# A retention and gated feed-forward block in fp32: the state update as four fp32 products, behind the scores

## The chip, the cores and the metric
The kernel runs on one core of one Trainium2 chip. Its metric is the device time of one execution in microseconds (us). TensorE (PE) multiplies, VectorE (DVE), ScalarE (ACT) and GpSimd (POOL) do the elementwise work, SyncE (SP) issues the DMAs.

## The reference, cut to what matters
Eight sequences of 512 tokens, 256 wide, go through a retention layer and a feed-forward layer, each with a residual and a layer norm. Retention has four heads, keys of 64 and values of 128. The reference works in chunks of 64 tokens; the state is what the change is about:

```python
attn = jnp.einsum('bhid,bhjd->bhij', qb, kb) * D[None]
o_intra = jnp.einsum('bhij,bhjd->bhid', attn, vb)
o_inter = jnp.einsum('bhid,bhde->bhie', qb * cross_q, S)
S_new = gC * S + jnp.einsum('bhjd,bhje->bhde', kb * cross_k, vb)
```

q and k are rotated (rotary embedding) first. The retained output is normed per head, gated with silu(x Wg), multiplied by Wo, added to x and layer-normed to x1. Then silu(x1 Wgate) * (x1 Wup) is multiplied by Wdown, added to x1 and layer-normed.

## The kernel before
**Tiling.** A tile is 128 tokens, four to a sequence, 32 in all. The decay factors are folded into the rotary tables, so that the state of a sequence is a plain sum of k^T v over its tiles. Every engine walks the same slots s = 0, 1, 2, ... (`walk_and_drain`), and in slot s it does the projections of tile s, the scores and retained products of tile s-1, the output projection of tile s-2, and the feed-forward of older tiles. Slots 0 to 11 and the last four are written out, the others are a loop over sequences; slots 0 to 7 (`natural`) also make q by rows, and 8 and later make it by columns. After slot 31 comes a `drain` for what is left. The order within a slot is written out by hand for each engine, and semaphores join the engines; within an engine all is in order.

**Split products.** Most products have each operand in two parts of type fp32r, high and low, and are the sum of three products high-high, high-low, low-high (`split_product`, whose matmul is L440). ScalarE casts the high part and GpSimd or VectorE subtracts to get the low part. Other products take fp32 operands as they are: the recall of the state (L555) and the scores (L558), both with 64 rows of contraction, and the retained products (L587), with 128. The profile shows each fp32 product as two pairs of weight load and matmul.

**The state.** `b_state` is a PSUM bank in which the update of a sequence accumulates over its first three tiles (the fourth has nobody to pass it to), 24 updates in all. Two heads share a product of 128 stationary columns of k and 256 columns of v, and only the diagonal halves of the result are used. So there are two pairs of heads by three split products, at the head of `to_projections` for tile s-2. `split_kv` casts k and v to `k_hi` and `v_hi` on ScalarE (L873, L874), and GpSimd makes `k_lo` and `v_lo` (L1516, L1517). `keep_state` on ScalarE copies the two diagonal halves into `state` (L925). The recall of the next tile waits for that (`state_kept`), and also for `y_ready` of the tile before its own, since it writes the PSUM banks that VectorE's `gated_output` reads (L1316). The v and k buffers have two slots each; who overwrites them waits for `kv_split`.

**PE's order in a slot** is: first projection, state update, feed-forward block 1, down projection, second projection, feed-forward block 2, recall and scores, transposes of x1 (L576) and of y (L615), gate projection (L454, L458), feed-forward block 0, output projection, retained products (L587), transposes of q and k (L468). Block 0 waits for the low part of x1 transposed (L1295) and the output projection for that of y (L1304), both made by VectorE from what ScalarE has cast (L885, L903).

Of the kernel before, what the change touches and what calls it, by code (L numbers as in the profile page):

```python
# [77 lines left out]
def build_block(nc, xT, x, w_proj, w_o, gn, w_ffn, rope, rope_by_row, out):  # L78
# [6 lines left out]
    with ExitStack() as ctx:  # L85
        def sb(name, shape, dt=F32):
            return ctx.enter_context(nc.sbuf_tensor(name, shape, dt))
# [4 lines left out]
        def sem(name):  # L92
            return ctx.enter_context(nc.semaphore(name))
# [13 lines left out]
        v_sb = sb("v_sb", [P, 2, V])  # L107
        v_hi, v_lo = sb("v_hi", [P, V], F32R), sb("v_lo", [P, V], F32R)

# [28 lines left out]
        qkT = sb("qkT", [P, 4, P])  # L138
        k_hi, k_lo = sb("k_hi", [P, 256], F32R), sb("k_lo", [P, 256], F32R)
        attn = sb("attn", [P, H, P])  # L140
# [84 lines left out]
        v_copied, g_gated = sem("v_copied"), sem("g_gated")  # L225
        kv_high, kv_split = sem("kv_high"), sem("kv_split")
        scores_done, masked = sem("scores_done"), sem("masked")
# [185 lines left out]
        def _(pe):  # L413
# [178 lines left out]
            def update_state(s, q, t):  # L592

                n, (qn, tn) = s - 2, back(q, t, 2)
                if exists(n) and tn < TS - 1:
                    if tn == 0 and exists(n - 2):
                        pe.wait_ge(state_kept, states_to(qn, tn) - 1)
                    pe.wait_ge(kv_split, states_to(qn, tn))
                    for pr in range(2):
                        cols, vals = slice(pr * P, (pr + 1) * P), slice(pr * 256, (pr + 1) * 256)  # L600
                        mm = split_product(b_state[:, vals], [(k_hi[:, cols], k_lo[:, cols])],
                                           [(v_hi[:, vals], v_lo[:, vals])], begun=(tn > 0 or pr > 0),
                                           more=(tn < TS - 2))
                    mm.then_inc(state_done, 1)
# [88 lines left out]
            def to_projections(s, q, t, wide):  # L693
                q1, t1 = q, t - 1
                update_state(s, q, t)
                gate_up_block(s - 1, q1, t1, 1, wide)
                down(s - 1, q1, t1, wide)
                if natural(s):
                    project(s, q, t, 1, v_done)
                else:  # L700
                    keys_and_queries(s, q, t)
                if is_slot(s, 0):
                    warm(FILL)
                gate_up_block(s - 1, q1, t1, 2, wide)
                recall_and_score(s, q, t)
                turn_x1(s, q, t)
                turn_y(s, q, t)
                project(s, q, t, 2, g_done)
# [18 lines left out]
            def drain(wide):  # L727

                q = NSEQ
                at = lambda t: (NT + t, q, t)  # L730
                update_state(*at(0))
                gate_up_block(*at(-1), 1, wide)
# [64 lines left out]
        def _(act):  # L797
# [58 lines left out]
            def copy_v(s, q, t):  # L856

                if exists(s):
                    act.wait_ge(v_done, s + 1)
                    if exists(s - 2):  # L860
                        act.wait_ge(o_done, s - 1)

                        act.wait_ge(kv_split, states_to(*back(q, t, 2)))
                    act.copy(v_sb[:, t % 2], v_bank(s, t)[:]).then_inc(v_copied, 1)

            def split_kv(s, q, t):

                if exists(s) and t < TS - 1:
                    act.wait_ge(rotated, s + 1)
                    act.wait_ge(v_copied, s + 1)  # L870
                    if exists(s - 1):
                        act.wait_ge(state_done, states_to(*back(q, t, 1)))
                    act.copy(k_hi[:], qk[:, t % 2, 256:512])  # L873
                    act.copy(v_hi[:], v_sb[:, t % 2]).then_inc(kv_high, 1)  # L874

# [42 lines left out]
            def keep_state(s, q, t):  # L918

                qn, tn = back(q, t, 1)  # L920
                if exists(s - 1) and tn < TS - 1:
                    act.wait_ge(state_done, states_to(qn, tn))
                    for a in range(2):
                        rows = slice(a * DK, (a + 1) * DK)
                        last = act.copy(state[rows], b_state[rows].rearrange(  # L925
                            "p (c n) -> p c n", c=2)[:, :, a * DV:(a + 1) * DV])
                    last.then_inc(state_kept, 1)

# [45 lines left out]
            def steady_slot(s, q, t):  # L974
# [6 lines left out]
                split_h(s - 1, t - 1, 0)  # L981
                split_kv(*prev)
                split_h(s - 1, t - 1, 1)
# [18 lines left out]
            def slot(s, q, t, ahead):  # L1002
# [17 lines left out]
                if is_slot(s, 1):  # L1020
                    split_xT(s + 2, *back(q, t, -2))
                    copy_v(s, q, t)
                    split_kv(s - 1, *back(q, t, 1))
                    split_ffn(0)
                elif is_slot(s, FFN_LAG) or is_slot(s, FFN_LAG + 1):
                    split_xT(s + 2, *back(q, t, -2))
                    copy_v(s, q, t)
                    if is_slot(s, FFN_LAG):
                        sum_low_ffn(3)
                    else:  # L1030
                        split_h(s - 1, t - 1, 1)
                        keep_x1(s, q, t)
                        split_kv(s - 1, *back(q, t, 1))
                else:
                    keep_x1(s, q, t)
                    split_h(s - 1, t - 1, 1)
                    split_kv(s - 1, *back(q, t, 1))
                    if ahead:
                        split_xT(s + 2, *back(q, t, -2))
                    copy_v(s, q, t)  # L1040
# [61 lines left out]
        def _(dve):  # L1102
# [59 lines left out]
            def rotate(s, q, t):  # L1162

                if exists(s):
# [3 lines left out]
                    if exists(s - 2):  # L1168
                        dve.wait_ge(qkT_done, s - 1)
                        dve.wait_ge(kv_split, states_to(*back(q, t, 2)))  # L1170
                    for e, sign in ((0, ALU.subtract), (1, ALU.add)):
# [28 lines left out]
            def sum_k(s, q, t):  # L1200

                if exists(s):
# [4 lines left out]
                    dve.wait_ge(qkT_done, s - 1)  # L1207
                    dve.wait_ge(kv_split, states_to(*back(q, t, 2)))
                    for e, sign in ((0, ALU.subtract), (1, ALU.add)):
# [270 lines left out]
        def _(pool):  # L1480
# [30 lines left out]

            def split_kv(s, q, t):

                if exists(s) and t < TS - 1:
                    pool.wait_ge(kv_high, states_to(q, t))
                    pool.tensor_tensor(k_lo[:], qk[:, t % 2, 256:512], k_hi[:].bitcast(F32), ALU.subtract)  # L1516
                    pool.tensor_tensor(v_lo[:], v_sb[:, t % 2], v_hi[:].bitcast(F32), ALU.subtract).then_inc(kv_split, 1)  # L1517

            def rms_norm(s, q, t):
# [37 lines left out]
            def steady_slot(s, q, t):  # L1557
# [3 lines left out]
                split_h(s - 1, t - 1, 0)  # L1561
                split_kv(*prev)
                split_h(s - 1, t - 1, 1)
# [7 lines left out]
            def slot(s, q, t, ahead):  # L1571
# [7 lines left out]
                split_h(s - 1, t - 1, 1)  # L1579
                split_kv(*before)  # L1580
                if ahead:
# [67 lines left out]
```

## Time and profile before

| | us |
|---|---|
| median of 3 runs | 443.9 (443.34 to 444.12) |
| profiled execution, its own time | 444.02 |
| its span, first to last instruction | 442.2 |
| PE busy (matmuls) | 428.2, 97% |
| PE weight loads | 400.4, 91% |
| VectorE busy | 302.1, 68% |
| ScalarE busy | 295.7, 67% |
| GpSimd busy | 238.9, 54% |

In the chain that ended last PE has 85% of the span, VectorE 8%, and 3% are time in which the engine waited for nothing that the profile shows. A row of the trace is one group of instructions in order of time: its start, its length, the engine, the line of the kernel, what is written and read, the tile of the array (rows*columns), the shape, the count, and in brackets the idle time before it and what ended it. Matmuls overlap, so that the length of one (0.27 to 0.28 us) is longer than the step from one to the next (0.11 us); the cost of a group is the step from its start to the start of the next.

### The profile page before, as it was taken

The page shows a single profiled execution, that of the slowest core. Times are in us where ns is not written, and L with a number is a line of the kernel's source. Part 1 is how long each engine was busy: PE and PEld are TensorE (multiplying, and loading weights), DVE is VectorE, ACT ScalarE, POOL GpSimd, SP SyncE. Part 2 cuts the span into 40 slices and gives each one's busy share as a digit, 9 for nine tenths or more (in the row PEclk, how much of TensorE's full clock was granted, in tenths as well). Part 3 has the DMA queues.
Part 4 walks back from the last instruction along what each step waited for, and adds up shares of the span by engine and source line. Part 5 has one row for each costly group of instructions (what it writes and reads, how often), then busy time and mean ns, then how long its engine had stood idle before and what let it go on. Part 6 is the DMA issues. An engine that isn't in the chain of part 4 may idle for free.

```text
span 442.2 us, 10997 instructions
## 1 busy us (share of the span) xinstructions
PE 428.2 (97%) x3552; PEld 400.4 (91%) x3552; DVE 302.1 (68%) x857; ACT 295.7 (67%) x891; POOL 238.9 (54%) x381
## 2 busy tenths in 40 slices
PE   7989999999999999999999999999999999999994
PEld 3878889999999999999999999999999999999983
DVE  4989566657766776666776667677666667766774
ACT  5678766657766767765776676686676667665541
POOL 2654255755555465453766446564655546554564
PEclk9999999999999999999999999999999999999998
DMA  7931000011100111110111101011110000100011
GB/s 241 363 134 50 0 29 22 24 38 37 38 11 27 37 38 38 37 37 0 36 36 36 36 27 44 0 36 36 36 36 13 15 22 14 38 12 13 14 38 39
DMA packets 16228, 19.60 MB, mean 44 GB/s; under 512 B 1472, under 2 KB 13760, under 8 KB 16192
## 3 DMA queue, kind: packets, MB, share of 16 engines
q1 hardware_dynamic: 16192, 19.14, 13.2%
q8 instruction: 20, 0.33, 0.3%
q14 instruction: 16, 0.13, 0.1%
HBM read 14.94 MB, written 4.19 MB: 43 GB/s over the span
## 4 chain that ended last, share of the span: by engine, by line
PE 85%; DVE 8%; issue 3%; POOL 1%; ACT 1%; DMA 1%; SPq 0%; POOLq 0%; DVEq 0%; ACTq 0%
PE b_rows L440 28%; PE b_ffn L440 18%; PE b_rows L458 8%; PE b_rows L454 6%; PE b_head L587 6%; PE b_head L555 3%; PE b_state L440 3%; PE b_head L558 3%; PE b_turn L615 3%; PE b_ffn L576 2%; PE b_turn L468 2%; DVE y L1316 1%; DMA wf_int<-in_w_proj 1%; DVE qk L1172 1%; DVE rot_s L1159 1%
## 5 line engine op out<-in xcount | busy, mean ns | idle before, releaser
L1509 POOL TENSOR_TENSOR h_lo<-wf_int,h_hi 128x256 fp32r<-128x256 f32 x96 | 71.0, 740 | 76.5 <-ACT h_hi L951 76.2
L440 PE MATMUL b_ffn<-x1T_hi,wf_hi 128*128 128x256 f32 x384 | 93.2, 279 | 1.0 <-DVE x1T_lo L1295 1.0
L440 PE MATMUL b_ffn<-x1T_lo,wf_hi 128*128 128x256 f32 x384 | 92.5, 278 | 0.0
L440 PEld LDWEIGHTS b_ffn<-x1T_hi,wf_hi 128*128 128x128 f32 x384 | 72.2, 188 | 2.1 <-DVE x1T_lo L1295 1.6
L440 PEld LDWEIGHTS b_ffn<-x1T_lo,wf_hi 128*128 128x128 f32 x384 | 72.3, 188 | 0.3
L915 ACT ACTIVATE sq<-b_head 128x128 f32<-128x128 f32 x124 | 34.4, 277 | 54.7 <-PE b_head L587 51.7
L1534 POOL TENSOR_TENSOR ve<-mv,eps 128x1 f32<-128x1 f32 x64 | 14.2, 222 | 93.7 <-DVE mv L1337 87.3
L940 ACT ACTIVATE wf_int<-b_ffn 128x256 f32<-128x256 f32 x96 | 36.8, 383 | 32.8 <-PE b_ffn L440 32.6
L951 ACT CAST h_hi<-wf_int 128x256 fp32r<-128x256 f32 x96 | 38.8, 405 | 19.1 <-DVE wf_int L1249 18.2
L1328 DVE TENSOR_TENSOR z<-b_rows,x_sb 128x256 f32<-128x256 f32 x32 | 13.5, 423 | 55.4 <-PE b_rows L440 55.4
L1249 DVE TENSOR_TENSOR wf_int<-b_ffn,wf_int 128x256 f32<-128x256 f32 x96 | 40.1, 418 | 15.5 <-ACT wf_int L940 11.2
L440 PE MATMUL b_rows<-wf_hi,h_hi 128*128 128x256 f32 x192 | 45.6, 278 | 0.3 <-POOL h_lo L1509 0.3
L440 PE MATMUL b_rows<-wf_hi,h_lo 128*128 128x256 f32 x192 | 45.3, 277 | 0.0
L1316 DVE SCALAR_TENSOR_TENSOR y<-b_head,rms,g_sb 128x128 f32<-128x128 f32 x124 | 34.9, 343 | 10.4 <-POOL rms L1528 9.9
L1536 POOL TENSOR_TENSOR rs<-ve,half_neg 128x1 f32<-128x1 f32 x64 | 34.9, 545 | 5.0
L1528 POOL TENSOR_TENSOR rms<-ms_eps,half_neg 128x4 f32<-128x4 f32 x32 | 36.0, 1124 | 2.5
L440 PE MATMUL b_rows<-wo_hi,yT_hi 128*128 128x256 f32 x128 | 35.7, 279 | 1.1 <-DVE yT_lo L1304 1.1
L440 PEld LDWEIGHTS b_rows<-wf_hi,h_hi 128*128 128x128 f32 x192 | 36.1, 188 | 0.5 <-POOL h_lo L1509 0.5
L440 PEld LDWEIGHTS b_rows<-wf_hi,h_lo 128*128 128x128 f32 x192 | 36.1, 188 | 0.0
L458 PE MATMUL b_rows<-wp_hi,xT_lo 128*128 128x256 f32 x144 | 36.0, 277 | 0.0
L440 PE MATMUL b_rows<-wo_lo,yT_hi 128*128 128x256 f32 x128 | 35.4, 276 | 0.0
L440 PE MATMUL b_rows<-wo_hi,yT_lo 128*128 128x256 f32 x128 | 35.4, 276 | 0.0
(154 smaller groups left out, 1320.2 us busy)
## 6 DMA issues: line engine op xcount, KB each, us to landing
xT_raw<-in_xT SPq DMA_DIRECT2D x16, 256.0 KB, 3.1
x_sb<-in_x SPq DMA_DIRECT2D x16, 256.0 KB, 2.7
out<-wf_int SPq DMA_DIRECT2D x32, 128.0 KB, 1.7
wf_int<-in_w_ffn SPq DMA_DIRECT2D x6, 384.0 KB, 7.6
wf_int<-in_w_proj SPq DMA_DIRECT2D x6, 256.0 KB, 5.2
rope_sb<-in_rope SPq DMA_DIRECT2D x4, 256.0 KB, 6.6
rope_q<-in_rope_by_row SPq DMA_DIRECT2D x2, 512.0 KB, 9.4
wo_raw<-in_w_o SPq DMA_DIRECT2D x1, 512.0 KB, 6.8
```

Of the source, the lines that this page charges most:

```text
L440: mm = pe.matmul(dst, a, b, start=(i == 0 and j == 0 and not begun), stop=(i == n - 1 and j == len(passes) - 1 and not more), skip_group_c ...
L454: pe.matmul(dst[:], a, b, start=i == 0, stop=False, skip_group_check=True)
L458: mm = pe.matmul(dst[:, cols], a, b[:, cols], start=False, stop=i == n - 1, skip_group_check=True)
L587: mm = pe.matmul(o_of(n, h), attn[:, h, :], v_sb[:, tn % 2, h * DV:(h + 1) * DV], start=False, stop=True, skip_group_check=True)
L915: act.activation(sq[:], o_of(n, h), ACT.Square, scale=float(DV) ** -0.5, accum_out=ms[:, tn % 2, h:h + 1]).then_inc(squared, 1)
L940: act.activation(act_g[:, u], b_ffn[u][:, 0:256], ACT.Silu, scale=SCALE).then_inc(silu_done[j], 1)
L951: act.copy(h_hi[:, ((t - FFN_LAG) // 2) % 2, hb], h_full[:, u]).then_inc(h_high[j], 1)
L1249: dve.tensor_tensor(h_full[:, u], b_ffn[u][:, 256:512], act_g[:, u], ALU.mult).then_inc(h_ready[j], 1)
L1316: last = dve.scalar_tensor_tensor(y[:, cols], o_of(n, h), rms[:, tn % 2, h:h + 1], g_sb[:, tn % 2, cols], ALU.mult, ALU.mult)
L1509: pool.tensor_tensor(h_lo[:, ring, hb], h_full[:, u], h_hi[:, ring, hb].bitcast(F32), ALU.subtract).then_inc(h_split[j], 1)
L1528: pool.tensor_tensor(rms[:, tn % 2], ms_eps[:, tn % 2], half_neg[:], ALU.pow).then_inc(rms_ready, 1)
L1536: pool.tensor_tensor(rs, ve, half_neg[:, 0:1], ALU.pow).then_inc(rstd, 1)
```

## The change
The state update becomes four fp32 products, one for each head: 128 rows, the head's 64 columns of k as the stationary operand, its 128 columns of v moving. The output of head h goes to partitions 0 to 63 or 64 to 127 (`half(h)`) and to the left or right 128 columns of what it uses of the bank. It is issued behind `recall_and_score` of the same slot for tile s-1, where it was issued at the head of the slot for tile s-2. `split_kv` is gone on both engines with its four tiles and two semaphores. `keep_state` is one copy of 128 partitions instead of two of 64. Where `kv_split` guarded the buffers of k and v, `state_done` does.

```diff
             def update_state(s, q, t):
 
-                n, (qn, tn) = s - 2, back(q, t, 2)
+                n, (qn, tn) = s - 1, back(q, t, 1)
                 if exists(n) and tn < TS - 1:
                     if tn == 0 and exists(n - 2):
                         pe.wait_ge(state_kept, states_to(qn, tn) - 1)
-                    pe.wait_ge(kv_split, states_to(qn, tn))
-                    for pr in range(2):
-                        cols, vals = slice(pr * P, (pr + 1) * P), slice(pr * 256, (pr + 1) * 256)
-                        mm = split_product(b_state[:, vals], [(k_hi[:, cols], k_lo[:, cols])],
-                                           [(v_hi[:, vals], v_lo[:, vals])], begun=(tn > 0 or pr > 0),
-                                           more=(tn < TS - 2))
+                    pe.wait_ge(rotated, n + 1)
+                    pe.wait_ge(v_copied, n + 1)
+                    for h in range(H):
+                        mm = pe.matmul(b_state[half(h), (h // 2) * DV:(h // 2 + 1) * DV],
+                                       qk[:, tn % 2, 256 + h * DK:256 + (h + 1) * DK],
+                                       v_sb[:, tn % 2, h * DV:(h + 1) * DV],
+                                       start=(tn == 0 and h < 2), stop=tn == TS - 2, skip_group_check=True)
                     mm.then_inc(state_done, 1)
...
             def to_projections(s, q, t, wide):
                 q1, t1 = q, t - 1
-                update_state(s, q, t)
                 gate_up_block(s - 1, q1, t1, 1, wide)
...
                 recall_and_score(s, q, t)
+                update_state(s, q, t)
                 turn_x1(s, q, t)
...
-                        act.wait_ge(kv_split, states_to(*back(q, t, 2)))
+                        act.wait_ge(state_done, states_to(*back(q, t, 2)))
                     act.copy(v_sb[:, t % 2], v_bank(s, t)[:]).then_inc(v_copied, 1)
-
-            def split_kv(s, q, t):
-
-                if exists(s) and t < TS - 1:
-                    act.wait_ge(rotated, s + 1)
-                    act.wait_ge(v_copied, s + 1)
-                    if exists(s - 1):
-                        act.wait_ge(state_done, states_to(*back(q, t, 1)))
-                    act.copy(k_hi[:], qk[:, t % 2, 256:512])
-                    act.copy(v_hi[:], v_sb[:, t % 2]).then_inc(kv_high, 1)
...
                 if exists(s - 1) and tn < TS - 1:
                     act.wait_ge(state_done, states_to(qn, tn))
-                    for a in range(2):
-                        rows = slice(a * DK, (a + 1) * DK)
-                        last = act.copy(state[rows], b_state[rows].rearrange(
-                            "p (c n) -> p c n", c=2)[:, :, a * DV:(a + 1) * DV])
-                    last.then_inc(state_kept, 1)
+                    act.copy(state[:], b_state[:, 0:2 * DV].rearrange("p (c n) -> p c n", c=2)).then_inc(state_kept, 1)
...
-            def split_kv(s, q, t):
-
-                if exists(s) and t < TS - 1:
-                    pool.wait_ge(kv_high, states_to(q, t))
-                    pool.tensor_tensor(k_lo[:], qk[:, t % 2, 256:512], k_hi[:].bitcast(F32), ALU.subtract)
-                    pool.tensor_tensor(v_lo[:], v_sb[:, t % 2], v_hi[:].bitcast(F32), ALU.subtract).then_inc(kv_split, 1)
```

In the drain the update of tile 30, which stood at its head, is likewise gone: slot 31 does it. VectorE's `rotate` and `sum_k`, which write k, wait for `state_done` of the tile two before instead of `kv_split`.

## Rows read from the trace of the kernel before

**Rows 1.** The page: busy time by engine, and granted clock in 40 slices.
```profile
PE 428.2 (97%) x3552; PEld 400.4 (91%) x3552; DVE 302.1 (68%) x857; ACT 295.7 (67%) x891; POOL 238.9 (54%) x381
...
PEclk9999999999999999999999999999999999999998
```

**Rows 2.** The timeline, PE, of slot 19: first of six update products, and next block.
```profile
236.13 0.28 PE L440 MATMUL b_state<-v_hi,k_hi 128*128 128x256 f32 x1
...
236.81 0.28 PE L440 MATMUL b_ffn<-x1T_hi,wf_hi 128*128 128x256 f32 x1
```

**Rows 3.** The timeline, PE: retained products of a tile, and what follows.
```profile
233.64 1.05 PE L587 MATMUL b_head<-v_sb,attn 128*128 128x128 f32 x8
...
234.53 0.38 PE L468 MATMUL b_turn<-ident,qk 128*128 128x128 f32 x2
```

**Rows 4.** The timeline, PE: last feed-forward product, recall, scores, x1 transposes.
```profile
241.26 0.28 PE L440 MATMUL b_ffn<-x1T_lo,wf_hi 128*128 128x256 f32 x1
...
241.47 0.71 PE L555 MATMUL b_head<-state,qT 64*128 64x128 f32 x8
...
242.02 0.61 PE L558 MATMUL b_head<-qT,qkT 64*128 64x128 f32 x8
...
242.56 0.44 PE L576 MATMUL b_ffn<-ident,x 128*128 128x128 f32 x2
```

**Rows 5.** The timeline, a steady slot: y, and the scores that wait for it.
```profile
264.75 1.12 DVE L1316 SCALAR_TENSOR_TENSOR y<-b_head,rms,g_sb 128x128 f32<-128x128 f32 x4 [0.45 <-POOL rms L1528]
...
267.41 0.72 PE L558 MATMUL b_head<-qT,qkT 64*128 64x128 f32 x8
```

**Rows 6.** The timeline of slot 4: y, the rotation's additions, the recall.
```profile
43.73 1.11 DVE L1316 SCALAR_TENSOR_TENSOR y<-b_head,rms,g_sb 128x128 f32<-128x128 f32 x4
...
44.77 0.75 DVE L1172 TENSOR_TENSOR qk<-rot_c,rot_s 128x256 f32<-128x256 f32 x2
...
45.20 0.71 PE L555 MATMUL b_head<-state,qkT 64*128 64x128 f32 x8 [1.04 <-DVE y L1316]
```

**Rows 7.** The timeline at the head of the drain: y, and the last recall.
```profile
406.58 1.13 DVE L1316 SCALAR_TENSOR_TENSOR y<-b_head,rms,g_sb 128x128 f32<-128x128 f32 x4 [0.96 <-POOL rms L1528]
...
407.92 0.71 PE L555 MATMUL b_head<-state,qT 64*128 64x128 f32 x8
```

**Rows 8.** By tile, ns min/median/max, first and last start: removed casts, split and copy.
```profile
L873 ACT CAST k_hi<-qk x24: 401/408/437, 16.4 to 394.8; 128x256 fp32r<-128x256 f32 x24
...
L874 ACT CAST v_hi<-v_sb x24: 613/622/648, 16.8 to 395.1; 128x512 fp32r<-128x512 f32 x24
L1517 POOL TENSOR_TENSOR v_lo<-v_sb,v_hi x24: 1267/1296/1731, 18.2 to 396.5; 128x512 fp32r<-128x512 f32 x24
...
L925 ACT COPY state<-b_state x48: 365/368/372, 21.7 to 405.7; 64x256 f32<-64x256 f32 x48
```

**Rows 9.** The timeline of slot 2: PE's two stalls, and what VectorE and GpSimd do.
```profile
24.21 1.27 POOL L1517 TENSOR_TENSOR v_lo<-v_sb,v_hi 128x512 fp32r<-128x512 f32 x1
24.63 2.00 DVE L1172 TENSOR_TENSOR qk<-rot_c,rot_s 128x256 f32<-128x256 f32 x2
...
24.77 0.66 PE L615 MATMUL b_turn<-ident,y 128*128 128x128 f32 x4 [0.57 <-DVE y L1316]
...
26.43 0.40 PE L440 MATMUL b_rows<-wp_hi,xT_lo 128*128 128x512 f32 x1
...
27.95 0.39 PE L440 MATMUL b_rows<-wo_hi,yT_hi 128*128 128x256 f32 x1 [1.12 <-DVE yT_lo L1304]
```

**Rows 10.** The timeline of slot 5: the cast of v, and PE's stall.
```profile
58.53 0.62 ACT L874 CAST v_hi<-v_sb 128x512 fp32r<-128x512 f32 x1
...
59.92 0.40 PE L440 MATMUL b_rows<-wp_hi,xT_lo 128*128 128x512 f32 x1
...
60.93 0.39 PE L440 MATMUL b_ffn<-x1T_hi,wf_hi 128*128 128x256 f32 x1 [0.61 <-DVE x1T_lo L1295]
```

**Rows 11.** The timeline of slot 9: PE's stall.
```profile
113.74 0.38 PE L440 MATMUL b_ffn<-x1T_hi,wf_hi 128*128 128x256 f32 x1 [0.37 <-DVE x1T_lo L1295]
```

More of the change, by code:

```diff
@@ L107, in build_block @@
         v_sb = sb("v_sb", [P, 2, V])
-        v_hi, v_lo = sb("v_hi", [P, V], F32R), sb("v_lo", [P, V], F32R)
         state = sb("state", [P, 2, DV])
@@ L138, in build_block @@
         qkT = sb("qkT", [P, 4, P])
-        k_hi, k_lo = sb("k_hi", [P, 256], F32R), sb("k_lo", [P, 256], F32R)
         attn = sb("attn", [P, H, P])
@@ L225, in build_block @@
         v_copied, g_gated = sem("v_copied"), sem("g_gated")
-        kv_high, kv_split = sem("kv_high"), sem("kv_split")
         scores_done, masked = sem("scores_done"), sem("masked")
@@ L730, in drain @@
                 at = lambda t: (NT + t, q, t)
-                update_state(*at(0))
                 gate_up_block(*at(-1), 1, wide)
@@ L981, in steady_slot @@
                 split_h(s - 1, t - 1, 0)
-                split_kv(*prev)
                 split_h(s - 1, t - 1, 1)
@@ L1022, in slot @@
                     copy_v(s, q, t)
-                    split_kv(s - 1, *back(q, t, 1))
                     split_ffn(0)
@@ L1032, in slot @@
                         keep_x1(s, q, t)
-                        split_kv(s - 1, *back(q, t, 1))
                 else:
@@ L1036, in slot @@
                     split_h(s - 1, t - 1, 1)
-                    split_kv(s - 1, *back(q, t, 1))
                     if ahead:
@@ L1169, in rotate @@
                         dve.wait_ge(qkT_done, s - 1)
-                        dve.wait_ge(kv_split, states_to(*back(q, t, 2)))
+                        dve.wait_ge(state_done, states_to(*back(q, t, 2)))
                     for e, sign in ((0, ALU.subtract), (1, ALU.add)):
@@ L1207, in sum_k @@
                     dve.wait_ge(qkT_done, s - 1)
-                    dve.wait_ge(kv_split, states_to(*back(q, t, 2)))
+                    dve.wait_ge(state_done, states_to(*back(q, t, 2)))
                     for e, sign in ((0, ALU.subtract), (1, ALU.add)):
@@ L1561, in steady_slot @@
                 split_h(s - 1, t - 1, 0)
-                split_kv(*prev)
                 split_h(s - 1, t - 1, 1)
@@ L1579, in slot @@
                 split_h(s - 1, t - 1, 1)
-                split_kv(*before)
                 if ahead:
```

## The prediction, made before the changed kernel ran

> **What bounds the kernel now.** I read the page first. TensorE (PE) is busy for 428.2 of the span of 442.2 us, at the full granted clock in nearly every slice; VectorE, ScalarE and GpSimd are busy for 54 to 68% [rows 1]. So work taken off ScalarE or GpSimd is worth nothing by itself: it counts only where PE waits for them. The profiled execution took 444.02 us, 1.8 us more than its span, and the median of the runs shown is 443.9 us. I sum against the profiled one and take 0.1 us off, which is less than anything below.
>
> Next I read PE's order of time in a steady slot. A product of 128 stationary columns and 256 moving ones in the split type follows the one before it after 0.113 us: six of them, the state update of before, stand from 236.13 to the next block at 236.81, 0.68 us [rows 2]. The weight loads lie beside them. The fp32 products of the retained values (four products, recorded as eight pairs of load and product, 128 stationary and 128 moving columns) stand from 233.64 to 234.53, so 0.89 us, 0.111 us a record [rows 3]. The fp32 products of 64 rows, which alternate between the upper and the lower half of the partitions, are quicker: eight records of the scores take from 242.02 to the x1 transposes at 242.56, where one at a time at 0.111 us they would take 0.89 us; the recall's eight take from 241.47 to 242.02 [rows 4]. Two heads run side by side there, and eight records cost about four steps.
>
> The same rows show what it costs to change the shape of tile. The last product of 128 rows begins at 241.26, would be followed after 0.113 us, and the first of 64 rows begins at 241.47: 0.10 us lost [rows 4]. The recall group also takes 0.55 us where four steps of 0.11 would be 0.44, so its first load is not hidden: another 0.1 us. A change of shape costs about 0.2 us.
>
> **The change part by part.** (1) The six split products go: 0.68 us for each of the 24 tiles that update the state (three of four in eight sequences) [rows 2].
>
> (2) Four fp32 products of 128 rows and 64 stationary columns come, behind the scores. No row of before shows this shape. The output of the even heads lies in partitions 0 to 63 and that of the odd in 64 to 127, so neighbours in the order use different column halves of the array, as the scores' neighbours use different row halves. Ends: if halves of columns run side by side as halves of rows do, the eight records take what the recall takes after a change of shape, 0.55 us [rows 4]. If they don't, they take 0.89 us [rows 3]. The change of shape between scores and x1 transposes exists already; now there are two. The second costs 0.10 us at its leaving edge (its entering edge is in the 0.55): 0.65 us with pairs. At the lower end a load of half the columns is hidden sooner and the group takes 0.55 us in all; at the upper end (no pairs, full change) 0.89 + 0.2 = 1.09 us. I take 0.64 us, nearest to the recall, the one group that is fp32, comes after a change of shape and alternates halves. So 24 x (0.64 - 0.68) = -1.0 us.
>
> On this the Trainium skill, TensorEngine Tiling (Array Packing), Key Properties, says that a change of tiling mode, not of tile, drains the engine; the trace agrees, by the 0.10 us ahead of the recall. TensorE: Matmul & The Clock Gate, Measured speedup vs the span model, gives 2.38 times for three column tiles, about what row tiles give, though it doesn't name fp32 there. The sum above does not use that figure.
>
> (3) The update moves from the head of the slot after next to the middle of the next one. Its waits are for the rotated k and the copied v of the previous tile, both of which are older than the scores, so nothing queues behind them. The recall waits for the kept state, and that now comes a whole slot earlier. ScalarE's next copy of v and VectorE's sum of k, which overwrite what the update reads, now wait for the update itself instead of the splits; it stands a slot ahead of them, so nothing is queued behind those waits. But the recall also waits for VectorE's y of the tile before, and the 0.68 us that stood ahead of it is gone. In the steady slots y has slack: it ends at 265.87 where the scores begin at 267.41, and 1.5 us is the smallest slack of them [rows 5]; 0.68 us comes off that and nothing waits. At two places y is already last. In slot 4 y runs from 43.73 for 1.11 us and PE, idle for 1.04 us, begins the recall at 45.20 [rows 6]. At the head of the drain y ends at 407.71 and the recall begins at 407.92 [rows 7]. There the update stood in the shadow of the wait; y is timed by the previous slot's retained products, which the new update pushes back. So each of the two loses the 0.68 us that part 1 counts as saved: +1.4 us.
>
> (4) ScalarE loses two casts (0.408 and 0.622 us) and one of two copies of the state (0.368 us) a tile, 1.4 us; GpSimd loses 1.296 us and the shorter split of k [rows 8]. Over the kernel that is 34 us of ScalarE and more of GpSimd, nearly all of it hidden. It shows where PE waits, early:
> - Slot 2. PE stands from 26.43 to 27.95 where a product of 512 columns takes about 0.23 us, for VectorE's low part of y, and before that 0.57 us for y itself [rows 9]. VectorE is late because its two additions of the rotation took 2.00 us from 24.63, while GpSimd's split of v ran from 24.21 for 1.27 us; the same two took 0.75 us from 44.77 [rows 6, 9]. Without the split of v I give back the 1.25 us and a little at the stall before: -1.4 us of 1.9. What is late then is the gate projection and the remaining y chain.
> - Slot 5. PE waits until 60.93 for the low part of x1, whose high part ScalarE copies only behind the cast of v at 58.53 and a gate [rows 10]. The wait is about 0.8 us (last product at 59.92, so 1.01 less 0.23). ScalarE is 1.0 us earlier: -0.8 us.
> - Slot 9. 0.37 us of idle before 113.74, for the same part of x1, to which I add the 0.1 us that the product ahead of it ran over its step [rows 11]: -0.5 us.
> Together -2.7 us. Bounds: 0 if another chain takes over at each, -3.2 us if all of it goes.
>
> The Trainium skill, SBUF — State Buffer, Who interferes with whom, states that a VectorE instruction with two inputs in SBUF contends with a GpSimd instruction that reads SBUF. The trace agrees: 2.00 against 0.75 us. The sum takes it from those rows.
>
> **Sum**: 444.0 - 1.0 + 1.4 - 2.7 = 441.7 us; taken from the median 441.6, and I say 441.7.
>
> **The rivals.**
> A. Pairs, but the start gives nothing back: the stalls are VectorE's, and its queue in slots 2 to 5 also holds the weight splits. 444.0 - 1.0 + 1.4 = 444.4 us. For it: y in slot 4 has no relief from this change. Against it: 2.00 against 0.75 us.
> B. Column halves do not run side by side, and no change of shape is paid: 0.89 us an update, 24 x 0.21 = +5.0, with the rest +3.7: 447.7 us. For it: the retained products are fp32 of 128 rows and run one at a time [rows 3]; two column halves want two streams of all 128 rows, where two row halves share one. It decides as soon as an update takes more than 0.74 us, where 24 x 0.06 eats the net gain at the waits.
> C. They don't, and the change of shape is paid: 1.09 us, 24 x 0.41 = +9.8, with the rest +8.5: 452.5 us. This is the one that I fear most, slower by 1.9%.
> D. Weight loads of column tiles are not hidden at all: a record then costs the exposed step at the start of the recall, 0.2 us; 8 x 0.2 + 0.2 = 1.8 us an update, 24 x 1.1 = +27, with the rest 470 us. Against it: in every row of the split products and of rows 3 the load of 128 rows lies beside the product before it. The Trainium skill, TensorE: Matmul & The Clock Gate, Measured speedup vs the span model, says that loads overlap products in flight only where the row group differs, and here it does not differ; by that rule D would come. The trace disagrees with the rule for whole tiles, since steps of 0.113 us leave no room for a load.
>
> **Chances.** Forecast 0.57, A 0.13, B 0.13, C 0.15, D 0.02. The forecast's own range is 439.5 (updates of 0.55 us) to 443.5. The whole range runs to B and what lies around it, 450.0, and leaves out C, D and a small tail, 0.2 together. A difference under 0.2% (0.9 us, so 443.0 to 444.8) can't be told from none here. Faster: 0.57 less a tail of 0.03, 0.54. Same: that tail and most of A, 0.11. Slower: the rest of A, B, C, D, 0.35.
>
> **What would show it.** Eight records of the state update in about 0.55 us with starts in close pairs: pairing right; spread evenly by 0.11: B or C. The step from the last score to the first update and from the last update to the x1 transposes, each some 0.2 us: the drain. An unchanged wait near 45 that grows to about 1.7 us, and the same at the head of the drain: part 3 right. VectorE's rotation at 0.75 us in slot 2, and stalls gone at about 27, 60 and 113: part 4 right. Spans of the steady sequences (16 updates and more) that move by more than 0.3 us each are the pairing and nothing else.

## The result, and the profile after

The changed kernel takes 439.59 us (median of four executions, 439.12 to 439.67) where the kernel before takes 443.62 (four, 443.21 to 444.12): a ratio of 0.9906, interval 0.9894 to 0.9918. It is faster by 0.9%, as forecast in direction, and inside the range, but by 4.0 us where the sum gave 2.3. The profiled execution took 439.12 us, the quickest of its four; the one of before took 444.02, 0.4 us over its median. So 4.9 us lie between the two profiles, and some 0.9 of them is spread between executions.

The page after, the part that answers to [rows 1]:

```profile
PE 424.6 (97%) x3600; PEld 393.6 (90%) x3600; DVE 296.6 (68%) x857; ACT 265.8 (61%) x819; POOL 189.0 (43%) x333
...
PEclk9999999999999999999999999999999999999998
...
PE 92%; DVE 2%; POOL 1%; issue 1%; DMA 1%; ACT 1%; SPq 0%; POOLq 0%; DVEq 0%; ACTq 0%
```

ScalarE has lost 30 us and GpSimd 50, PE 3.6. The third line is the chain that ended last: VectorE's share of it fell from 8 to 2%. The granted clock is what it was.

The state update of a steady slot, PE in order of time, between the last feed-forward products and the x1 transposes; it answers to [rows 2, 4]:

```profile
236.87 0.28 PE L437 MATMUL b_ffn<-x1T_lo,wf_hi 128*128 128x256 f32 x1
237.09 0.72 PE L552 MATMUL b_head<-state,qT 64*128 64x128 f32 x8
237.63 0.61 PE L555 MATMUL b_head<-qT,qkT 64*128 64x128 f32 x8
238.18 0.66 PE L598 MATMUL b_state<-v_sb,qk 128*64 128x128 f32 x8
238.76 0.33 PE L573 MATMUL b_ffn<-ident,x 128*128 128x128 f32 x1
```

The scores still take 0.54 us to the next group, and the update 0.59 to the x1 transposes: this, leaving edge included, is its whole cost. The starts of its eight matmuls are 0, 6, 161, 167, 269, 276, 378 and 386 ns: four close pairs, and 0.20 us behind the last. The recall ahead has the same picture, except that its second pair starts at 213 ns. The view by tile, with min, median and max in ns, shows the difference:

```profile
L598 PEld LDWEIGHTS b_state<-v_sb,qk x192: 132/137/138, 16.2 to 393.2; 128*64 128x64 f32 x192
L598 PE MATMUL b_state<-v_sb,qk x192: 272/273/325, 16.2 to 393.3; 128*64 128x128 f32 x192
L910 ACT COPY state<-b_state x24: 384/395/398, 21.6 to 400.7; 128x256 f32<-128x256 f32 x24
```

A load of 64 columns takes 137 ns where those of 128 columns take 188, and the first step of the group, the one place where a load isn't hidden, is 0.05 us shorter than the recall's.

**Where the time went.** The retained products of a tile follow in both kernels on the same stretch of work, so the shift of their start places the gain. The change of those starts is a staircase: from the tile with number 11 on it falls by 0.28 us in each sequence, exactly, from -3.92 to -5.04 at tile 27. That is three updates that cost 0.093 us less each, and nothing else.

| stretch | shift, us | of it updates | of it waits and stalls |
|---|---|---|---|
| weights arrive, to the first scores | -0.34 | | -0.34 |
| to tile 3 | -1.53 | -0.28 | slot 4's recall +0.59, stalls of slots 1 to 3 -1.84 |
| to tile 7 | -1.17 | -0.28 | slot 5's stall -0.89 |
| to tile 11 | -0.88 | -0.28 | slot 9's stall -0.60 |
| to tile 27 | -1.12 | -1.12 | none |
| to tile 31 | +0.42 | -0.28 | the drain's recall +0.70 |
| rest of the drain | -0.27 | | -0.27 |
| sum | -4.89 | -2.24 | -2.65 |

The two waits that grow, PE, in slot 4 and at the head of the drain; they answer to [rows 6, 7]:

```profile
41.32 0.40 PE L437 MATMUL b_rows<-wp_hi,xT_lo 128*128 128x512 f32 x1
...
41.98 1.11 DVE L1295 SCALAR_TENSOR_TENSOR y<-b_head,rms,g_sb 128x128 f32<-128x128 f32 x4
...
43.35 0.71 PE L552 MATMUL b_head<-state,qkT 64*128 64x128 f32 x8 [1.64 <-DVE y L1295]
```

```profile
402.17 0.28 PE L437 MATMUL b_ffn<-x1T_lo,wf_hi 128*128 128x256 f32 x1
...
403.28 0.72 PE L552 MATMUL b_head<-state,qT 64*128 64x128 f32 x8 [0.82 <-issue]
```

The idle time ahead of slot 4's recall went from 1.04 to 1.64 us, behind the same 1.11 us of y. In the drain the step to the recall went from 0.40 to 1.11 us; y ended at 403.06, so the "issue" of the row is the wait for y all the same.

And slot 2, which answers to [rows 9]:

```profile
23.69 0.75 DVE L1151 TENSOR_TENSOR qk<-rot_c,rot_s 128x256 f32<-128x256 f32 x2
...
25.49 0.69 DVE L1283 TENSOR_TENSOR yT_lo<-b_turn,yT_hi 128x512 fp32r<-128x512 f32 x1 [0.38 <-ACT yT_hi L890]
...
25.84 0.40 PE L437 MATMUL b_rows<-wp_hi,xT_lo 128*128 128x512 f32 x1
...
26.24 0.39 PE L437 MATMUL b_rows<-wo_hi,yT_hi 128*128 128x256 f32 x1
```

VectorE's two additions take 0.75 us where they took 2.00, and the step to the output projection is 0.40 us where it was 1.52. The wait for y ahead of its transposes is gone too: the step from the last score to what follows is 0.20 us, where the transposes followed after 0.85, and the update now stands there. The stalls of [rows 10, 11] are gone.

### The profile page after: what moved, and what is told of

It reads as the page before. It is cut to its first block, busy times and chain, and to the rows that moved or that the text cites. A ratio compares the mean times of both kernels' runs of the same rounds, so it can differ in the third digit from the quotient of the medians.

```text
span 437.3 us, 10954 instructions
## 1 busy us (share of the span) xinstructions
PE 424.6 (97%) x3600; PEld 393.6 (90%) x3600; DVE 296.6 (68%) x857; ACT 265.8 (61%) x819; POOL 189.0 (43%) x333
## 4 chain that ended last, share of the span: by engine, by line
PE 92%; DVE 2%; POOL 1%; issue 1%; DMA 1%; ACT 1%; SPq 0%; POOLq 0%; DVEq 0%; ACTq 0%
PE b_rows L437 32%; PE b_ffn L437 19%; PE b_rows L455 9%; PE b_rows L451 6%; PE b_head L584 6%; PE b_head L555 4%; PE b_head L552 3%; PE b_state L598 3%; PE b_turn L613 3%; PE b_ffn L573 2%; PE b_turn L465 2%; DMA wf_int<-in_w_proj 1%; POOL h_lo L1488 1%; DVE wf_lo L1096 0%; POOL rs L1508 0%
```

## Experiments: why an update costs 0.59 us

The prediction's mechanism was: two column halves of the array run side by side, as two row halves do, and a change of tile shape costs 0.2 us. Its reading of how was that the half must alternate from one product to the next. The expectations below number the theories: under Theory 1 alternation of neighbours is what makes the pairs. Its rival is that the pairs do not hang on the order.

**e1: the same products in another order.** Heads 0 and 2 go to the upper partitions, 1 and 3 to the lower, so neighbours now change half once instead of three times.

```diff
-                    for h in range(H):
+                    for h in (0, 2, 1, 3):
```

> The changed kernel with one line altered: the four update products go out in the order of heads 0, 2, 1, 3, so that neighbours share a half of the array's columns, where before they alternated. Theory 1 (the pairs in the trace are two heads side by side in the two halves of columns): heads 0 and 2 run one after the other, so do 1 and 3, and only one meeting of halves is left; the group of eight records grows from 0.59 us by two to three steps of 0.11 us, to 0.8 to 0.9 us, 24 x 0.27 = +6.5 us, 446 us. Rival 2 (the two records that lie 7 ns apart belong to one and the same product): the order of heads does not matter, 0.59 us and 439.6 us.

Measured: 439.69 us, 0.9907 of before (0.9888 to 0.9926). The update's rows:

```profile
238.21 0.67 PE L598 MATMUL b_state<-v_sb,qk 128*64 128x128 f32 x8
238.80 0.44 PE L573 MATMUL b_ffn<-ident,x 128*128 128x128 f32 x2
```

It takes 0.59 us as before, and the starts still come in pairs: 0, 14, 160, 175, 270, 284, 379 and 393 ns. Theory 1 missed by 6 us. The only thing that changed is the distance inside a pair, 14 ns instead of 7. This fits two streams, one for each half, each in its own order: in the new order the first matmul of the second half is the fourth behind the first of all, where it was the second. The trace doesn't name the head of a matmul, so that reading is inferred. What is shown is that the order of the heads is worth nothing.

**e7: all four heads to the same half.** This could mean that pairs have nothing to do with halves: the two matmuls of one fp32 product might pair with each other. So all four results go to partitions 0 to 63. The state of heads 1 and 3 is then not computed, while the work is of the same size.

```diff
-                        mm = pe.matmul(b_state[half(h), (h // 2) * DV:(h // 2 + 1) * DV],
+                        mm = pe.matmul(b_state[0:DK, (h // 2) * DV:(h // 2 + 1) * DV],
```

> The changed kernel with all four update products written to partitions 0 to 63, so that all use the same half of the array's columns (the state of the odd heads isn't computed, and the sums are wrong). Theory 8 (the two records of one fp32 product go side by side when its tile is half the array, whichever half): still 0.59 us an update, starts in pairs 7 ns apart, 439.6 us. Theory 1, what is left of it (alternating halves matter somewhere): more than 0.59 us, up to 0.9 us an update and 447 us.

Measured: 449.82 us in one execution.

```profile
244.15 1.09 PE L598 MATMUL b_state<-v_sb,qk 128*64 128x128 f32 x8
245.16 0.44 PE L573 MATMUL b_ffn<-ident,x 128*128 128x128 f32 x2
```

1.02 us (the two starts shown are rounded), with starts at 0, 160, 270, 379, 488, 597, 706 and 815 ns: one every 0.109 us behind the first step. A pair inside a product falls, and the halves are what makes pairs. Neighbours that write the same place in the bank are not what spreads them: if they stand in the order of issue, the fifth matmul belongs to another head and writes other columns than the fourth, and it follows by the same 0.109 us. 24 x (1.02 - 0.59) is 10.3 us, and 10.2 were measured. The group also prices rival C of the prediction (no pairs, change of shape paid): 449.8, where it said 452.5.

**e2: full tiles in fp32.** Is it the column tiles at all, or only the place and the missing splits? Two fp32 products of 128 stationary columns and 256 moving ones, behind the scores, as in before only with their diagonal halves used; ScalarE copies them in two pieces again.

```diff
-                    for h in range(H):
-                        mm = pe.matmul(b_state[half(h), (h // 2) * DV:(h // 2 + 1) * DV],
...
+                    for pr in range(2):
+                        mm = pe.matmul(b_state[:, pr * 256:(pr + 1) * 256],
+                                       qk[:, tn % 2, 256 + pr * P:256 + (pr + 1) * P],
+                                       v_sb[:, tn % 2, pr * 256:(pr + 1) * 256],
```

> The changed kernel with the update as two fp32 products of 128 columns of k and 256 of v (full tiles of the array, half of each result unused as in the kernel before), the state copied in two halves again. Theory 1 (what the update saves is the column halves): fp32 moving columns cost twice those of the split records, 4 records of 0.22 us each make 0.87 us instead of 0.59, and one change of shape fewer is in that already: 24 x 0.28 = +6.7 us, 446 us, and 0.2 us of PE more for each update than in the kernel before. Rival 3 (fp32 without split copies is itself the gain, a record costs 0.11 us whatever its columns): 0.45 us an update, 24 x -0.14, 436 us.

Measured: 448.92 us, 1.0109 of before (1.0092 to 1.0126).

```profile
243.76 1.13 PE L598 MATMUL b_state<-v_sb,qk 128*128 128x256 f32 x4
244.73 0.38 PE L573 MATMUL b_ffn<-ident,x 128*128 128x128 f32 x2
```

0.97 us an update: 24 x 0.38 = 9.1 us over the changed kernel, and 9.3 were measured. I had expected 446. A matmul of 256 moving columns in fp32 steps by 0.216 us, where the split type steps by 0.113 [rows 2], and the step behind the change of shape, 0.32 us here, was left out of my figure. So without the column tiles this change would have made the kernel slower.

## Experiments: the place

**e3: the four products back at the head of the slot.** All else as changed, the update for the tile two before, between the first projection and feed-forward block 1, and at the head of the drain.

```diff
-                n, (qn, tn) = s - 1, back(q, t, 1)
+                n, (qn, tn) = s - 2, back(q, t, 2)
...
             def to_projections(s, q, t, wide):
                 q1, t1 = q, t - 1
+                update_state(s, q, t)
...
                 recall_and_score(s, q, t)
-                update_state(s, q, t)
```

> The changed kernel with the update put back at the head of the slot, for the tile two before, and at the head of the drain; products unchanged. Theory 4 (the new place costs 0.7 us at slot 4 and 0.7 us at the head of the drain, where y is last, and saves one change of shape an update): the waits ahead of the recall near 42 and 402 us shrink by 0.7 us each, -1.4 us; the group now stands between full tiles and pays entering and leaving, about 0.1 us more each than next to the scores, +2.4 to +4.8 us; together 440.6 to 443.0 us. Rival 5 (the place is free, both ways): 439.6 us.

Measured: 445.84 us, 1.0041 of before (1.0026 to 1.0056): slower than before, and 6.3 us over the changed kernel. The steps to the recall went back, from 2.03 to 1.25 us in slot 4 and from 1.11 to 0.42 in the drain, as the prediction's part 3 has it, 1.5 us in all. The stall of slot 9 is back:

```profile
110.70 0.28 PE L455 MATMUL b_rows<-wp_hi,xT_lo 128*128 128x256 f32 x1
111.35 0.39 PE L437 MATMUL b_ffn<-x1T_hi,wf_hi 128*128 128x256 f32 x1 [0.37 <-DVE x1T_lo L1275]
```

So the updates lose more than 7 us together; a steady sequence loses 0.94, which is 0.31 for each update against the place behind the scores. The rows of one of them, PE:

```profile
248.78 0.28 PE L455 MATMUL b_rows<-wp_hi,xT_lo 128*128 128x256 f32 x1
248.99 0.66 PE L598 MATMUL b_state<-v_sb,qk 128*64 128x128 f32 x8
249.57 0.38 PE L437 MATMUL b_ffn<-x1T_hi,wf_hi 128*128 128x256 f32 x1
249.80 0.28 PE L437 MATMUL b_ffn<-x1T_lo,wf_hi 128*128 128x256 f32 x1
...
250.15 0.28 PE L437 MATMUL b_ffn<-x1T_hi,wf_hi 128*128 128x256 f32 x1
...
251.92 0.28 PE L437 MATMUL b_rows<-wf_hi,h_lo 128*128 128x256 f32 x1
```

The group itself is still 0.59 us. Going in costs 0.09 (0.206 us from 248.78 instead of 0.113). The first full tile behind it exposes a load, 0.22 instead of 0.113: 0.11 more. And then the full tiles step by 0.118 us instead of 0.113 up to the next feed-forward block: 15 steps from 250.15 to 251.92 make 1.77 us, 30 and more of them together 0.14. Block 2, which steps by 0.118 in the changed kernel, goes at 0.113 to 0.114 here but for its first two steps and gives 0.03 back. That is the 0.31. The granted clock is full there, so the slower rhythm isn't the clock's:

```profile
249.00:254.00 5.00, 5.00 (x46) 4.83 (x46) 3.79 (x12) 3.04 (x10) 3.35 (x6) 1.00 0.18 60
```

(The columns are busy times of PE, weight loads, VectorE, ScalarE and GpSimd, then the granted clock, 1.00.) The slower rhythm is no mark of the column tiles either. In e2, which has none, 26 full-tile products in a row have it in a slot with an update, 25 steps from the first of these rows to the second making 2.95 us:

```profile
246.09 0.28 PE L455 MATMUL b_rows<-wp_hi,xT_hi 128*128 128x256 f32 x1
...
249.04 0.28 PE L437 MATMUL b_rows<-wo_hi,yT_lo 128*128 128x256 f32 x1
```

So of the 0.31 the 0.20 at the two edges goes with the change of shape, and the cause of the rest is not shown. Behind the scores none of it is paid: the change of shape from scores to transposes was there before. I had expected 0.1 to 0.2 us for each update.

**e5: late at two places only.** The changed kernel loses 1.3 us at two recalls that wait for y. There the update can stand in the shadow of the wait, as it did in before, and everywhere else behind the scores.

```diff
+                if isinstance(s, int) and s in (4, NT):
+                    update_state(s, q, t, 1)
                 gate_up_block(s - 1, q1, t1, 1, wide)
...
-                update_state(s, q, t)
+                if not (isinstance(s, int) and s + 1 in (4, NT)):
+                    update_state(s, q, t)
...
                 at = lambda t: (NT + t, q, t)
+                update_state(*at(0), 1)
```

(The last argument makes the update that of the tile one further back.)

> The changed kernel with the update of two tiles issued later: that of tile 2 at the head of slot 4 and that of tile 30 at the head of the drain, as in the kernel before; all others behind the scores. Theory 4 (at these two places the update pushes back the retained products, by them y, and by it the recall): the wait ahead of the recall shrinks by 0.7 us at each, and each pays 0.3 us for standing between full tiles (as all of them did in the run with the update at the head of the slot): -0.8 us against the changed kernel, 438.8 us, the fastest version so far. Rival 5 (the waits there have another cause): unchanged, or 0.6 us slower for the dearer place.

> The changed kernel itself, as the measure for the run beside it on the same chip: 439.6 us, ratio to before 0.9906.

Measured: 438.66 us, 0.9880 of before (0.9864 to 0.9897). The changed kernel beside it on the same chip took 439.49, 0.9903 (0.9887 to 0.9920). So it gains 0.8 us and is the fastest version here, though the two intervals overlap. The profile shows the gain at the recall by itself:

```profile
41.40 0.40 PE L437 MATMUL b_rows<-wp_hi,xT_lo 128*128 128x512 f32 x1
42.66 0.71 PE L552 MATMUL b_head<-state,qkT 64*128 64x128 f32 x8 [0.85 <-DVE y L1299]
```

The two steps to the recall shrink by 0.78 and 0.69 us, 1.5 together. With the 0.31 us of e3 for each of the two updates that leaves 0.85, where 0.83 were measured, but the agreement is partly luck. Against the changed kernel's run beside it the update costs 0.20 more in slot 4, with no slower rhythm behind it, and 0.10 more at the head of the drain; later in the drain e5 steps by 0.118 us where the other steps by 0.113, and that costs 0.26. Together these leave 0.9 us.

## Experiments: the start

**e4: all four split copies kept, read by nobody.** ScalarE casts k and v, GpSimd subtracts, where they did in before; TensorE works as changed. What remains of the start-up gain belongs to the place; what goes belongs to the relief of ScalarE and GpSimd.

```diff
+            def split_kv(s, q, t):
+
+                if exists(s) and t < TS - 1:
+                    act.wait_ge(rotated, s + 1)
+                    act.wait_ge(v_copied, s + 1)
...
+                    act.copy(k_hi[:], qk[:, t % 2, 256:512])
+                    act.copy(v_hi[:], v_sb[:, t % 2]).then_inc(kv_high, 1)
```

> The changed kernel with the four split copies of k and v still made by ScalarE and GpSimd (nobody multiplies them), with the guards that they need. Theory 6 (some 3.4 us of the gain are stalls of the first ten slots that the splits caused): those stalls come back, at slots 2, 5 and 9, and the steady slots stay as they are: 443.0 us. Rival 7 (the start gained from the new place and the earlier kept state, not from the relief): 439.6 us.

Measured: 441.87 us, 0.9952 of before (0.9935 to 0.9968), 2.3 over the changed kernel, where I had expected 3.4. The steady sequences still gain 0.28 us each. Slot 2:

```profile
23.69 1.27 POOL L1516 TENSOR_TENSOR v_lo<-v_sb,v_hi 128x512 fp32r<-128x512 f32 x1
24.11 2.01 DVE L1170 TENSOR_TENSOR qk<-rot_c,rot_s 128x256 f32<-128x256 f32 x2
...
25.91 0.40 PE L440 MATMUL b_rows<-wp_hi,xT_lo 128*128 128x512 f32 x1
...
27.44 0.38 PE L440 MATMUL b_rows<-wo_hi,yT_hi 128*128 128x256 f32 x1 [1.14 <-DVE yT_lo L1303]
```

The additions and the stall are back as they were in [rows 9]: 2.01 and 1.53 us. A stall that before did not have stands in slot 3 (1.30 us), where the additions take 2.20 us beside the same split; so the 2.3 us is more than the splits cost before. GpSimd's split of v begins 0.24 us ahead of these additions, where in before it began 0.96 us behind them and they took 1.28. The stall of slot 9 stays away, and the step of slot 5 is 0.42 us instead of 1.01, where 0.23 is a step without a stall. With e3 this settles both. Slot 9 is the place alone: gone in e4, back in e3. In slot 5 the relief removes all of it (e3) and the place most (e4).

What the place does there can be read from the order. In slots 5 and 9 the kernel before has no update, since tile s-2 is the fourth of its sequence; the changed kernel has one, for tile s-1, ahead of the same wait for x1. Its 0.59 us stand in the wait: 1.01 - 0.59 is the 0.42 of e4, and the stall of slot 9 was shorter than that.

**e8 and e9: one engine's half each.** Which operation is it? e8 has only GpSimd's two subtractions, started without the casts (k - k and v - v), e9 only ScalarE's two casts.

```diff
-                    pool.tensor_tensor(k_lo[:], qk[:, t % 2, 256:512], k_hi[:].bitcast(F32), ALU.subtract)
+                    pool.tensor_tensor(k_lo[:], qk[:, t % 2, 256:512], qk[:, t % 2, 256:512], ALU.subtract)
```

> The changed kernel with GpSimd alone still doing the two subtractions of the size of the split's (fp32 k minus itself and v minus itself, for nobody), ScalarE's casts gone. Theory 9 (the 2.2 us that all four dead copies cost come from GpSimd's reads beside VectorE's additions in slots 2 and 3): the stalls near 26 and 37 us of that run are there, 441.5 us. Rival 10 (they come from ScalarE's casts): 439.8 us.

> The changed kernel with ScalarE alone still doing the two casts of k and v (for nobody), GpSimd's subtractions gone. GpSimd's dead work alone had cost 0.5 us, all four together 2.3 us. Theory 10 (the rest is ScalarE's: its casts push back what VectorE and PE wait for in slots 2 and 3): the stall near 26 us is 1.0 us or more and the one near 37 us too, 441.3 us. Theory 11 (the two need each other: the casts delay GpSimd's reads into VectorE's additions): near nothing here, 439.7 us.

Measured: e8 439.99 us, 0.9920 (0.9903 to 0.9936), so Theory 9 missed by 1.5 us; e9 439.42 us, 0.9897 (0.9881 to 0.9914). Slot 2 of e8, and below of e9:

```profile
22.56 1.04 POOL L1511 TENSOR_TENSOR v_lo<-v_sb 128x512 fp32r<-128x512 f32 x1
...
23.10 1.66 DVE L1164 TENSOR_TENSOR qk<-rot_c,rot_s 128x256 f32<-128x256 f32 x2
...
26.08 0.38 PE L440 MATMUL b_rows<-wo_hi,yT_hi 128*128 128x256 f32 x1 [0.47 <-DVE yT_lo L1297]
```

```profile
22.32 0.64 ACT L873 CAST v_hi<-v_sb 128x512 fp32r<-128x512 f32 x1
...
23.83 0.84 DVE L1168 TENSOR_TENSOR qk<-rot_c,rot_s 128x256 f32<-128x256 f32 x2
```

The casts alone cost nothing that the medians show (within 0.2 us), GpSimd alone costs 0.4 to 0.5, and together they cost 2.3. So the loss needs both. How, the rows of slot 1 show; the first two are of e4, the third is of the changed kernel:

```profile
16.96 0.74 POOL L1515 TENSOR_TENSOR k_lo<-qk,k_hi 128x256 fp32r<-128x256 f32 x1 [1.17 <-ACT v_hi L875]
18.28 2.18 DVE L1122 TENSOR_TENSOR wo_lo<-wo_raw,wo_hi 128x1024 fp32r<-128x1024 f32 x1
```

```profile
18.75 1.23 DVE L1104 TENSOR_TENSOR wo_lo<-wo_raw,wo_hi 128x1024 fp32r<-128x1024 f32 x1
```

GpSimd waits 1.17 us for the casts, and its splits then lie beside VectorE's of the weights, whose low part of wo takes 2.18 us instead of 1.23 (1.64 in e8). VectorE comes to slot 2 late: its additions begin 0.70 us behind the update there in e4, and 0.14 in e8. In slot 2 itself no cast holds GpSimd back; it goes on from rms to its splits without a gap in both. But in e4 it is only a third through its split of v when the additions begin, in e8 a half. In slot 3 it waits for the casts again, for 0.27 us. One reservation: e8's subtractions read one tile twice and are shorter (1.04 against 1.27 us), so a part of its mildness is that.

Slot 5 is the casts' own. With them alone the 0.42 us of e4 are there again, while e8 has a step without a stall; e9:

```profile
58.77 0.40 PE L440 MATMUL b_rows<-wp_hi,xT_lo 128*128 128x512 f32 x1
59.19 0.38 PE L440 MATMUL b_ffn<-x1T_hi,wf_hi 128*128 128x256 f32 x1
```

The Trainium skill, SBUF — State Buffer, Who interferes with whom, says of such a meeting that the order of issue, not the shape of the operation, decides who blocks. The rows agree in kind: where GpSimd was first in e4 its split kept its 1.27 us and the additions grew by 1.26. Only 0.85 us of that split lay beside them, though; GpSimd's next split, of x, followed at once, so the additions met both.

## Why the prediction was right or wrong

**Direction, and the mechanism of the update: right.** Column halves run side by side (e7), the pairs are there, and the rivals B, C and D with no pairs or bare loads fell. So did A: the start gave back more than a half of the net gain.

**The size: wrong, and the failed step is the cost of an update**, part 2, where it said "I take 0.64 us, nearest to the recall". Measured 0.59: 0.16 for the first step from pair to pair, twice 0.11, and 0.21 from the last pair to the transposes. The sum carried over the recall's first step, 0.21 us, which holds a load of 128 columns of 0.188 us; here the load has 64 columns and 0.137, and the step is 0.16. The text had named this ("a load of half the columns is hidden sooner") and used it for the lower end alone. Since the saving is a difference of two numbers near each other, 0.68 - 0.64, an error of 0.05 more than doubles it: 24 x 0.093 = 2.2 us instead of 1.0. The mechanism stands; what failed is the size of this term.

**Part 3, the exposed recalls: right.** +1.4 forecast, +0.59 and +0.70 measured; e3 and e5 take them back. y has slack in all other slots: the staircase has no other rise.

**Part 4, the start: right in place, short in size, half wrong in cause.** Slots 1 to 3 gave 1.84 us instead of 1.4. In slot 2 the stall gave 1.12 and the wait for y 0.65 (a step of 0.85 that is 0.20 now), of which I had counted only a little. The relief alone removes that wait (e3), the update in its new place a part of it (in e4 a step of 0.45 is left). I had also read only slot 2: VectorE was late there already from slot 1, where its low part of wo took 2.19 us beside GpSimd's splits and takes 1.23 now. Slots 5 and 9 gave 0.89 and 0.60 instead of 0.8 and 0.5, so the numbers were right, and for slot 9 by luck: I put both to ScalarE's lost cast, which holds for slot 5 (e8, e9), where the moved update alone would have filled most of it. Slot 9's is due to the moved update alone (e3, e4).

**Behind the sum.** Of the 2.0 us between 441.6 and 439.6 the update is 1.2, the start 0.6 and the recalls 0.1. The -0.34 us while weights arrive and the -0.27 at the end of the drain are of the size by which executions of one kernel differ: the same kernel run again as e6 has -0.64 at the first place and -0.05 at the second. I don't count them.

**What stays open.** Why full tiles step by 0.118 instead of 0.113 us in some stretches and not in others: over 30 products after the column tiles in e3, 26 in e2, block 2 of the kernels before and after, and the head of the drain of the changed kernel, where no tiled group stands ahead; and which head a matmul of a pair belongs to.

## What to carry to other kernels

Where a saving is the difference of two group costs near each other, cost the new group step by step, its first load and both edges each from its own row: the nearest group as a whole hides an error as large as the saving. Put work of a tiled shape beside work that changes shape already, since the same group cost 0.31 us more between full tiles in a steady slot, and 0.10 to 0.20 at the two places of e5. And before giving a relieved engine the credit for a stall, ask what else moved: one experiment that keeps the load and one that keeps the place tell them apart. Here slot 9 was the place alone, slot 2's long stall the load alone, and in slot 5 either removed most of it or all.

## What the runs showed of the hardware

- fp32 products of 64 stationary columns pair when they use different column halves: eight matmuls of 128 moving columns cost 0.59 us from their first start to the next group behind the scores, 1.02 on one half. They paired in both orders tried (starts 7 and 14 ns apart).
- A weight load of 64 columns took 137 ns, one of 128 columns 188. In e7 steps of 0.109 us leave no room for a bare load of 137 ns, though all loads go to the same rows and the same columns. The Trainium skill, TensorE: Matmul & The Clock Gate, The mechanism, says that a load overlaps products in flight only where the row group differs; the trace disagrees. It is the rule behind rival D, for which the prediction named another section of that page. The same section also lets a load into the background weight buffer go ahead of products in flight; that would fit these rows, but no run here shows which buffer a load goes to.
- Against its place behind the scores a tiled group between full tiles cost 0.09 us more going in and 0.11 for the first load behind it; from its last matmul to the next product it is 0.20 us in either place. Full tiles step by 0.113 or 0.118 us at full granted clock, also in a kernel without column tiles (e2), and over 30 products the slower step costs 0.14 us.
- Two additions of VectorE on 128 x 256 took 0.75 us alone, and 1.66 to 2.20 in slots 2 and 3 beside subtractions of GpSimd of which one had begun before them (1.53 in slot 3 of e8).
